# Router of 32: the chosen experts found by their order to the fourth value and place; the first expert's weights loaded and split during the router's phase

## What is computed

```python
# mixture: E = 8, TOPK = 2
scores = jax.nn.softmax(logits.astype(jnp.float32), axis=-1)
_, indices = jax.lax.top_k(scores + gate_bias, TOPK)
weights = jnp.take_along_axis(scores, indices, axis=1)
for e in range(E):
    y = y + _mlp(xt, w1[e], w2[e], w3[e]) * combine[:, e:e + 1]
z = _mlp(xt, sw1, sw2, sw3)
return (y + z).reshape(shape)
```

## Time and profile before

| | |
|---|---|
| three runs | 2774.49, 2777.86, 2784.76 us |
| the profiled execution: its time | 2785.57 us |
| its span | 2783.8 us |
| TensorE busy | 2443.3 us, 88% |
| VectorE busy | 2090.0 us, 75% |
| ScalarE busy | 1427.4 us, 51% |
| GpSimd busy | 656.4 us, 24% |
| f1: router's first matmul to first gate_up | 28.50 to 56.06 |
| f2: first gate_up | 628.5 |
| g1: router's first matmul to first gate_up | 1181.30 to 1213.76 |
| g2: first gate_up | 2501.0 |

### The profile page before, as it was taken

One profiled execution on the slowest core, in us unless ns is written; L12 is line 12 of the kernel. 1 busy time (PEld: TensorE's weight loads), 2 busy tenths in 40 slices (PEclk: granted clock), 3 DMA queues, 4 the chain that ended last, 5 costly groups with the idle time before them and its releaser, 6 DMA issues. The chain is left out here.

```text
span 2783.8 us, 38252 instructions
## 1 busy us (share of the span) xinstructions
PE 2443.3 (88%) x11980; PEld 1429.3 (51%) x11980; DVE 2090.0 (75%) x4150; ACT 1427.4 (51%) x3040; POOL 656.4 (24%) x701
## 2 busy tenths in 40 slices
PE   6995899949988999869998589999669899969998
PEld 4773333227756555457775422222136555437776
DVE  3994777538968999279996188888348899639998
ACT  2553356615521777246664136677521477516665
POOL 2334132213317000034443300000005200014443
PEclk8997799969989999879998779999878999969999
DMA  2212111012212000024442611010222000014443
GB/s 65 83 57 75 32 50 47 8 42 104 77 38 50 1 1 1 8 98 156 147 143 58 161 42 33 27 34 9 34 58 46 5 1 1 8 34 145 150 143 120
DMA packets 104848, 166.61 MB, mean 60 GB/s; under 512 B 55170, under 2 KB 77570, under 8 KB 92850
## 3 DMA queue, kind: packets, MB, share of 16 engines
q1 hardware_dynamic: 87812, 162.77, 18.6%
q10 hardware_dynamic: 16896, 2.10, 0.5%
HBM read 145.36 MB, written 12.78 MB: 57 GB/s over the span
## 5 line engine op out<-in xcount | busy, mean ns | idle before, releaser
L1529 DVE TENSOR_REDUCE b1x_maxima<-b1x_m_bank 128x1 f32<-128x512 f32 x512 | 318.9, 682 | 57.5 <-PE b1x_m_bank L1463 56.6
L1549 ACT ACTIVATE b1x_probs<-b1x_e_bank 128x1024 f32<-128x1024 f32 x256 | 248.3, 1021 | 142.0 <-PE b1x_e_bank L1480 141.9
L1529 DVE TENSOR_REDUCE a1x_maxima<-a1x_m_bank 128x1 f32<-128x512 f32 (+3 forms) x384 | 191.3, 548 | 60.3 <-PE a1x_m_bank L1466 31.4
L1549 ACT ACTIVATE a1x_probs<-a1x_e_bank 128x1024 f32<-128x1024 f32 (+1 forms) x192 | 146.1, 813 | 133.4 <-PE a1x_e_bank L1480 133.2
L1463 PE MATMUL b1x_m_bank<-b1a_k_slot,b1a_q_slot 96*128 96x512 bf16 x512 | 186.6, 404 | 11.1 <-DMA b1a_q_slot<-scratch_q_parts 10.8
L1480 PE MATMUL b1x_e_bank<-b1a_q_slot,b1a_k_slot 128*128 128x512 bf16 x512 | 153.6, 383 | 0.9 <-ACT b1x_probs L1549 0.4
L1463 PE MATMUL a1x_m_bank<-a1a_k_slot,a1a_q_slot 96*128 96x512 bf16 (+3 forms) x384 | 121.3, 354 | 21.6 <-POOL a1x_mask L1414 12.8
L1495 PE MATMUL b1x_o_bank<-b1x_probs,b1a_v_aug 128*32 128x512 f32 x1024 | 136.4, 605 | 0.7 <-ACT b1x_probs L1549 0.7
L1463 PEld LDWEIGHTS b1x_m_bank<-b1a_k_slot,b1a_q_slot 96*128 96x128 bf16 x512 | 41.6, 98 | 166.7 <-DVE b1x_maxima L1529 128.8
L632 ACT ACTIVATE g1e_high<-g1e_hidden 128x512 fp32r<-128x512 f32 x128 | 81.0, 633 | 89.9 <-DVE g1e_hidden L665 89.9
L632 ACT ACTIVATE g2e_high<-g2e_hidden 128x512 fp32r<-128x512 f32 x128 | 81.0, 633 | 89.4 <-DVE g2e_hidden L665 89.3
(11 more groups left out here) (564 smaller groups left out, 6628.1 us busy)
## 6 DMA issues: line engine op xcount, KB each, us to landing
g1e_share<-scratch_combine SPq DMA_DIRECT2D x32, 1024.0 KB, 4.8
g2e_share<-scratch_combine SPq DMA_DIRECT2D x32, 1024.0 KB, 4.8
f1e_share<-scratch_combine SPq DMA_DIRECT2D x9, 1024.0 KB, 4.8
f2e_share<-scratch_combine SPq DMA_DIRECT2D x9, 1024.0 KB, 4.9
b1e_window<-scratch_bias_table SPq DMA_DIRECT2D x16, 320.0 KB, 4.7
a1a_k_slot<-scratch_k_parts SPq DMA_DIRECT2D x24, 192.0 KB
a1a_q_slot<-scratch_q_parts SPq DMA_DIRECT2D x24, 192.0 KB
b1a_k_slot<-scratch_k_parts SPq DMA_DIRECT2D x24, 192.0 KB
```

The source lines that it names most:

```text
L1529: dve.tensor_reduce(maxima[:, k0 // NC, col:col + 1], bank[:, 0:width], AX, ALU.max).then_inc(m_taken, 1)
L1549: act.activation(probs[u % 2][:, 2 * pair:2 * pair + 2, 0:width], e_bank[pair][:, :, 0:width], ACT.Exp, scale=scale).then_inc(exp_done, 1)
```

## The change

The router of 32 experts no longer builds a matrix for each of the four places. It selects all four at once: an expert is chosen if its value is above the fourth value, or equal to it and its number is not above the fourth place. `hit` is 1 where the number is above the fourth place; `biased` becomes the distance to the fourth value; `combine` becomes 1 where hit times the smallest normal float is at most that distance. Exp is taken of all 32 distances to the largest value (`scores`), in a second call on ScalarE, and `combine` is multiplied by the inverse of the sum of the four and then by `scores`. The router of 8 is as it was. The row of ones is set only in the router of 8.

The tensors and semaphores of the experts' weights move to the phase around router and experts (`ExpertParts`). The first expert's weights are loaded at the start of the router's phase, rounded by ScalarE behind the copies of h, and subtracted by GpSimd behind h's. In the experts' phase SP first loads the first share; the loop of loads then runs from the second expert on.

```diff
-def router(nc, tag, sbuf, h, cut_h, gate, bias, combine_dram, E, K, softmax_first):
+class ExpertParts:
+    def __init__(self, phase, weights, halves):
...
+    def load(self, sp, k, slot):
+        sp.wait_ge(self.w_low_done, k + 1)
+        sp.dma_start(self.w[slot][:], self.weights[bass.ds(k, 1), :, 0:self.width].rearrange(
+            "e p c -> (e p) c")).then_inc(self.w_loaded[slot], 16)
+        sp.wait_ge(self.down_low_done, k + 1)
...
+    def load_first(self, sp):
+        sp.dma_start(self.w[0][:], self.weights[0, :, 0:self.width]).then_inc(self.w_loaded[0], 16)
+        sp.dma_start(self.w_down[0][:], self.weights[0, :, self.width:]).then_inc(self.down_loaded[0], 16)
+
+    def high_of_first(self, act):
+        act.wait_ge(self.w_loaded[0], 16)
+        act.activation(self.w_high[0][:], self.w[0][:], ACT.Copy).then_inc(self.w_high_done, 1)
+        act.wait_ge(self.down_loaded[0], 16)
+        act.activation(self.down_high[0][:], self.w_down[0][:], ACT.Copy).then_inc(self.down_high_done, 1)
+
+    def low_of_first(self, pool):
+        pool.sem_inc(self.w_low_done, 2)
+        pool.sem_inc(self.down_low_done, 2)
+        self.cut_weights(pool, 0, 0)
+        self.cut_down(pool, 0, 0)
+        pool.wait_ge(self.w_low_done, 3)
+        pool.wait_ge(self.down_low_done, 3)
...
+SMALLEST = 2.0 ** -126
...
+            parts.high_of_first(act)
             act.wait_ge(shifted, 1)
             if softmax_first:
                 act.activation(scores[:], biased[:], ACT.Exp).then_inc(exp_done, 1)
             else:
-                act.activation(picked[:, :, 0:K], top[:, :, 0:K], ACT.Exp).then_inc(exp_done, 1)
+                act.activation(picked[:, :, 0:K], picked[:, :, 0:K], ACT.Exp).then_inc(exp_done, 1)
+                act.wait_ge(all_shifted, 1)
+                act.activation(scores[:], scores[:], ACT.Exp).then_inc(exp_done, 1)
...
+            done(dve.tensor_copy(col[:], top[:, :, 0]))
+            dve.tensor_tensor(picked[:, :, 0:K], top[:, :, 0:K],
+                              col[:].unsqueeze(2).to_broadcast([128, NT, K]),
+                              ALU.subtract).then_inc(shifted, 1)
+            dve.tensor_tensor(scores[:], biased[:], over_experts(col[:]), ALU.subtract
+                              ).then_inc(all_shifted, 1)
+
+            done(dve.tensor_tensor(hit[:], over_tiles(sbuf["iota"][:, 0:E]), over_experts(placef[:, :, K - 1]),
+                                   ALU.is_gt))
+            done(dve.tensor_tensor(biased[:], biased[:], over_experts(top[:, :, K - 1]), ALU.subtract))
+            done(dve.scalar_tensor_tensor(out=combine[:].rearrange("p t e -> p (t e)"),
+                                          in0=hit[:].rearrange("p t e -> p (t e)"), scalar=SMALLEST,
+                                          in1=biased[:].rearrange("p t e -> p (t e)"), op0=ALU.mult,
+                                          op1=ALU.is_le))
+            dve.wait_ge(exp_done, 1)
+            done(dve.tensor_reduce(total[:], picked[:, :, 0:K], AX, ALU.add))
+            done(dve.reciprocal(total[:], total[:]))
+            done(dve.tensor_tensor(combine[:], combine[:], over_experts(total[:]), ALU.mult))
+            dve.wait_ge(exp_done, 2)
+            dve.tensor_tensor(combine[:], combine[:], scores[:], ALU.mult).then_inc(combine_done, 1)
...
         def _(pool):
-            pool.memset(ones[:], 1.0).then_inc(ones_set, 1)
-            pool.wait_ge(ones_set, 1)
+            if softmax_first:
+                pool.memset(ones[:], 1.0).then_inc(ones_set, 1)
+                pool.wait_ge(ones_set, 1)
...
+            parts.low_of_first(pool)
             pool.wait_ge(low_done, NCH)
...
         def _(sp):
+            parts.load_first(sp)
             if softmax_first:
...
-            with sp.Fori(0, pairs) as it:
-                for slot in range(2):
-                    load_weights(it * 2 + slot, slot)
-                    load_down(it * 2 + slot, slot)
-                    load_share(it, slot)
...
+            sp.dma_start(share[0][:], combine_dram[0:1, :].to_broadcast([128, T])
+                         ).then_inc(share_loaded[0], 16)
+            with sp.Fori(0, pairs - 1) as it:
+                for after in (1, 2):
+                    parts.load(sp, it * 2 + after, after % 2)
+                    load_share(it * 2 + after, after % 2)
+            for k in range(routed - 1, total):
+                parts.load(sp, k, k % 2)
+                load_share(k, k % 2)
```

More of the change, by code:

```diff
@@ L314, in router @@
+SMALLEST = 2.0 ** -126
+def router(nc, tag, sbuf, h, parts, gate, bias, combine_dram, E, K, softmax_first):
     with Phase(nc, tag) as p:
@@ L326, in router @@
         copied, stored, shifted = p.sem("copied"), p.sem("stored"), p.sem("shifted")
-        ones_set = p.sem("ones_set")
+        ones_set, all_shifted = p.sem("ones_set"), p.sem("all_shifted")
         high_done, low_done = p.sem("high_done"), p.sem("low_done")
@@ L392, in _ @@
             done(dve.tensor_copy(placef[:], place[:]))
[L393 to L410, removed]
@@ L411, in _ @@
-            dve.tensor_tensor(combine[:], combine[:], hit[:], ALU.add).then_inc(combine_done, 1)
+            if softmax_first:
+                for k in range(K):
+                    into = combine if k == 0 else hit
+                    done(dve.tensor_tensor(into[:], over_tiles(sbuf["iota"][:, 0:E]),
+                                           over_experts(placef[:, :, k]), ALU.is_equal))
+                    done(dve.tensor_tensor(into[:], into[:], scores[:], ALU.mult))
+                dve.tensor_tensor(combine[:], combine[:], hit[:], ALU.add).then_inc(combine_done, 1)
+                return
@@ L430, in _, with experts @@
             sp.wait_ge(stored, 32 if softmax_first else 16)
-def cut_parts(phase):
-    return phase.sb("h_high", [128, T], F32R), phase.sb("h_low", [128, T], F32R)
-def experts(nc, tag, sbuf, cut_h, x, weights, combine_dram, halves, routed, shared, inner=None):
+def experts(nc, tag, sbuf, parts, x, combine_dram, halves, routed, shared, inner=None):
     steps = NCH * halves
-    width, down_width = halves * 256, halves * 128
     pairs = routed // 2
@@ L456, in experts @@
         gate_up = [p.ps(f"gate_up{s}", [128, 2, NC]) for s in range(2)]
[L457 to L460, removed]
-        down_high = [p.sb(f"down_high{s}", [128, down_width], F32R) for s in range(2)]
-        down_low = [p.sb(f"down_low{s}", [128, down_width], F32R) for s in range(2)]
-        h_high, h_low = cut_h
+        w, w_down, w_high, w_low = parts.w, parts.w_down, parts.w_high, parts.w_low
+        down_high, down_low = parts.down_high, parts.down_low
+        h_high, h_low = parts.h_high, parts.h_low
         share = [p.sb(f"share{s}", [128, T]) for s in range(2)]
@@ L1907, in mixture @@
     with Phase(nc, tag) as p:
-        cut_h = cut_parts(p)
-        router(nc, tag + "r", sbuf, h, cut_h, sbuf["moe_gate"], sbuf["moe_bias"][:], dram["combine8"],
+        parts = ExpertParts(p, dram["moe_w"], halves=2)
+        router(nc, tag + "r", sbuf, h, parts, sbuf["moe_gate"], sbuf["moe_bias"][:], dram["combine8"],
                8, 2, True)
-        experts(nc, tag + "e", sbuf, cut_h, x, dram["moe_w"], dram["combine8"], halves=2, routed=8,
+        experts(nc, tag + "e", sbuf, parts, x, dram["combine8"], halves=2, routed=8,
                 shared=True)
```

77 lines of the change are left out of this document (37 added, 40 removed).

## The result

| | before | after |
|---|---|---|
| timed runs, median | 2777.23 us (4 runs) | 2747.7 us (4 runs, 2743.61 to 2748.36) |
| ratio | | 0.9886, 95% interval 0.9865 to 0.9908 |
| profiled execution: time, span | 2785.57, 2783.8 us | 2748.36, 2746.6 us |
| mean granted clock of TensorE | 0.915 | 0.925 |

The kernel became 29.5 us faster by the medians. Forecast were 21.5 us less, with a range from 2747 to 2767 us. So the sign and most of the size were right, and a part was missed. Where the forecast had its terms, the profile after reads as follows.

What follows compares the result with a forecast made beforehand. The kernel was taken as a chain of phases with barriers, each bound by the engine the others wait for. -8.4 - 13.7 - 1.6 + 2.2 = -21.5 us from 2777.9 gave 2756.4 us, range 2747 to 2767.

Steps and rivals of the forecast that it cites:

- Router's tail: 32-way router in g1 and g2: VectorE's tail falls from 9.29 to 5.07 us, -8.4 us together.
- Start of the experts and clock: Experts' start in four phases: TensorE's idle time vanishes, -13.7 us, and its clock rises sooner, -1.6 us.
- idle term: TensorE's waits between zeroing and gate_up vanish: 2.84, 4.4, 4.0 and 2.5 us, together -13.7 us.
- the clock: Experts' start: zeroing takes over gate_up's half-speed time, 0.4 us in each of four phases, -1.6 us, from 0 to -3.7.
- The port: Routers of f1 and f2: GpSimd's moved subtraction holds VectorE's scores-plus-bias sum, 1.1 us each, +2.2 us, bounds 0 to +4.0.
- Exp of f1: f1's router: ScalarE's roundings and table load end 0.8 us ahead of Exp, so priced at 0.
- one of the signs named for being wrong: f1's router: Exp starting late behind its table load would show the prediction wrong.
- The share was in time: Rival at the experts' start: first share lands 1.1 us late in each phase, 4.3 us given back, 2760.7 us; chance 0.12.
- The loop of experts ran as before: Rival in g1 and g2: one more share product per expert meets GpSimd, 34 us slower, 2790 us; chance 0.04.
- GpSimd held VectorE for one subtraction, not for two: Rival in f1 and f2: VectorE waits for both subtractions, 2.0 us each instead of 1.1, 2758.2 us; chance 0.04.
- The start did move: Rival at the experts' start: something unnamed holds the first products, only the router's part and its cost remain, 2771.7 us; chance 0.05.
- what an edit is worth is read in its own phases: Whole kernel: with a barrier between phases, an edit's value is read in its own phases, from which engine the others await.

Runs made afterwards that it cites:

- e9: Kernel after, with GpSimd's subtraction of the first weights in the 8-way routers held until VectorE has written scores plus bias; 2741.03 us, ratio 0.9854.
- e2: The changed kernel measured once more, with no edit; 2752.6 us, ratio 0.9915 to the kernel before.
- e5: Kernel before, with a VectorE addition of 128x1024 that TensorE waits for at the head of norms a1n, g1n and g2n; 2767.31 us, ratio 0.9951.
- e7: Kernel after, with a pause (VectorE addition of 128x1280) ahead of the norm g2n alone; 2742.14 us, ratio 0.9864.
- e11: Kernel after, with one zero product ahead of each powers group in centred norms, GpSimd's first-weight subtractions held, and a 1024 pause in g2n; 2734.35 us, ratio 0.9833.
- e8: Kernel after, with one TensorE product of zeros, 128x512, ahead of each group of powers in the mean-subtracting norms; 2737.09 us, ratio 0.9839.

## Why the prediction was right and wrong

- *Router's tail.* Forecast -4.2 in each of g1 and g2; the profile of after has -4.4 in g1, and the stretch from the first maximum to the turned rows is 4.3 shorter in both. The forms cost what the nearest rows had said.
- *Start of the experts and clock.* Forecast -13.7 and -1.6, together -15.3. The time from zeroing to the first Silu, over four phases, went from 33.1 to 16.8: -16.3. The sum is near, but not by its terms. From the start of the zeroing to gate_up it was 21.3 us over the four phases and is 5.0, -16.2 alone; from gate_up to the first Silu it was 11.9 and is 11.7. So the idle term was too small by 2.5, because it counted from the end of the zeroing's row, and the clock gave next to nothing up to there. What it gave behind it no run tells apart. That the two terms together came near is luck.
- *The port.* Forecast +2.2. The held sum costs 0.94 in each of f1 and f2, +1.9; by the stages it is 0.35 or 0.8 a phase, by which profiles one compares. The rule that the Trainium skill gives (SBUF — State Buffer, "Who interferes with whom") holds here: with GpSimd out of the way the same operation is 0.29 us (e9), with it 1.23.
- *Exp of f1.* Priced at 0, and in e2's execution it is. In the profile after it is 0.5 us late behind its table load, one of the signs named for being wrong, as in that execution the logits were ready at 33.2, before ScalarE was.
- *The rivals.* The share was in time in g1 and g2, and late by 0.1 us in f1 and 0.3 in f2, where the rival had 1.1 each. The loop of experts ran as before: the share's product in g1 has 693 ns as its median and 1228 as its maximum over 128, where the earlier trace rows have 694 and 1228. GpSimd held VectorE for one subtraction, not for two. The start did move.
- *What failed* is the step that read the value of an edit in its own phases alone, "what an edit is worth is read in its own phases", and a sum with no term for anything behind them. The own phases came out at -23.5 (forecast -21.5, with bounds from -26 to -17). But a phase that ends sooner moves the start of what follows, and each norm that follows takes 5 to 8 us more or less, by whether its clock rises soon. In the profiled pair that was a1's and b1's, 13 us, and by the ratio 8 us of the whole lie outside the own phases. The trace of the kernel before had it: a1's norm at clock 0.50 for 18 us with TensorE busy. I looked at windows in g1's experts only, and the range had nothing for the norms but the scatter of three runs. How many norms are fast changes from one execution to the next, so that this measurement fell just outside the range and e2 inside it is chance.

What stays open: which places are the good ones can't be told for a new kernel. The runs show that a pause of 1.2 to 1.5 us ahead of a slow norm made it fast, five times of five (e5, e7, e11), and that in a1, g1, b1 and g2 the clock rises either 3 to 5 us or 18 to 23 us after the first product, and not what the chip looks at. In f1's norm the column of the granted clock is of no use at first: it stands at 1.00 from the start, also in the profile of before, where each product takes 1061 ns. There the length of the products tells. It wasn't tried whether a longer pause turns a norm back, nor a later start without the idle time. The gain of e11 over e8 isn't larger than the error either.

## What to carry to other kernels

Where TensorE's clock falls and rises again within each phase, as here, an edit that moves a phase by a microsecond can win or lose several in phases it doesn't touch. List the stretches where TensorE is busy at 0.50, count each as a term of its own price with either sign, and widen the range by it. And compare own phases of two profiles before explaining a total: here they repeat within 2 us where the total moves by 20. Preparing the first item of a loop in the phase ahead was worth the whole idle time at the loop's start and 0.6 us more in each phase. Count such a gap from start to start in the profile, not from the idle time in the brackets. What it costs is looked for where the moved instruction meets another engine's two-input operation.

## What I had not expected of the hardware

- A dense norm can run at the lower clock for 18 us: 8 products of 1061 ns each instead of 592 once the clock has risen.
- A pure delay made a kernel faster: three pauses of 1.2 us took 0.5% off the kernel before (e5).
- After its early rise the clock can fall back within the norm with TensorE busy: from 224.0 to 227.5 in a1's norm of the kernel after, which took 13.2 us instead of 11.5.
- Operations of VectorE on other data, with no wait between, start before the one ahead is through: 0.60 us apart for 0.68 us of length.
